# Routing stage of a graph and mixture-of-experts kernel: VectorE's work per group cut in four parts and reordered, scatter places from two products and a scan, expert weights turned one unit per group

## The reference

```
x = x + gnn(layernorm(x), edge_attr_16, edge_attr_4, ..., src, dst)   # x: 6250 x 256, 200000 edges, 8 heads
flat   = layernorm(x)
probs  = softmax(flat @ router_w.T)                                   # 8 experts
topk_probs, topk_idx = top_k(probs, 2)
topk_probs = topk_probs / (sum(topk_probs) + 1e-09)
gates  = einsum("nk,nke->ne", topk_probs, one_hot(topk_idx, 8))
h      = silu(flat @ w1[e].T) * (flat @ w3[e].T)                      # w1, w3: 8 x 682 x 256
y[e]   = h @ w2[e].T                                                  # w2: 8 x 256 x 682
x      = x + sum over e of gates[:, e] * y[e]
```

## Time and profile before

| | |
|---|---|
| median of 3 runs | 4229.73 us |
| the profiled execution, its own time | 4242.61 us |
| its span | 4240.8 us |
| the stage between loop and experts | 3059.6 to 3309.0 us of the span |
| busy share of the span: PE, PEld, DVE, ACT, POOL | 74%, 56%, 47%, 38%, 44% |
| scatters on POOL (L1298) | 98, busy 106.8 us, idle before them 131.0 us |
| weight transposes on PE (L1428) | 192, busy 50.5 us |
| router matmuls on PE (L1405) | 196, busy 45.3 us |
| granted TensorE clock in the stage | 0.50 |

### The profile page before, as it was taken

One profiled execution on the slowest core, in us unless ns is written; L12 is line 12 of the kernel. 1 busy time (PEld: TensorE's weight loads), 2 busy tenths in 40 slices (PEclk: granted clock), 3 DMA queues, 4 the chain that ended last, 5 costly groups with the idle time before them and its releaser, 6 DMA issues. The chain is left out here.

```text
span 4240.8 us, 66247 instructions
## 1 busy us (share of the span) xinstructions
PE 3155.8 (74%) x12650; PEld 2393.4 (56%) x12651; DVE 1982.3 (47%) x5336; ACT 1615.5 (38%) x3611; POOL 1861.5 (44%) x1906
## 2 busy tenths in 40 slices
PE   2532787777777777777777777777766699999997
PEld 1221665555565656555555665565555477777775
DVE  5730555555555555555555555555744122222221
ACT  2311544444444444444444444444422122222221
POOL 0005455556555555555555555555245111111111
PEclk9865667777767777777777677767755899999998
DMA  7744444444444444444444444446553321221113
GB/s 217 253 134 120 122 128 124 125 127 126 125 125 127 128 123 127 131 128 126 125 127 124 125 125 125 125 125 118 87 176 133 101 32 30 32 31 31 31 31 82
DMA packets 311626, 480.40 MB, mean 113 GB/s; under 512 B 164215, under 2 KB 239811, under 8 KB 302670
## 3 DMA queue, kind: packets, MB, share of 16 engines
q0 software_dynamic: 100848, 285.40, 27.4%
q1 hardware_dynamic: 208606, 193.39, 15.2%
q10 hardware_dynamic: 2000, 0.06, 0.0%
HBM read 408.92 MB, written 76.12 MB: 114 GB/s over the span
## 5 line engine op out<-in xcount | busy, mean ns | idle before, releaser
L838 POOL DMA_INDIRECT rows<-table,idx x1664 | 1577.9, 948 | 1141.0 <-issue 488.8
L881 PE MATMUL ps_acc<-rows,hot 128*128 128x264 f32 x3328 | 1274.3, 521 | 396.9 <-DVE acc L1169 342.9
L881 PEld LDWEIGHTS ps_acc<-rows,hot 128*128 128x128 f32 x3328 | 767.9, 255 | 535.1 <-issue 422.0
L1169 DVE TENSOR_TENSOR acc<-acc,ps_acc 128x264 f32 x832 | 356.7, 429 | 1047.0 <-remote 459.5
L866 PEld LDWEIGHTS ps_term<-er,hot_t 128*128 128x128 f32 x3328 | 619.1, 249 | 285.6 <-issue 235.6
L866 PE MATMUL ps_term<-er,hot_t 128*128 x3328 | 608.2, 314 | 125.6 <-issue 93.3
L1155 DVE TENSOR_TENSOR rows<-rows,ps_p 128x512 f32<-128x512 f32 x832 | 565.7, 680 | 2.4 <-ACT ps_p L984 0.5
L973 ACT ACTIVATE hot<-iota_row,neg_rel 128x128 f32<-128x128 f32 x1664 | 545.8, 388 | 4.8 <-PE ps_acc L881 4.6
L1713 PE MATMUL ps_h<-w,acc 128*128 x1680 | 530.8, 459 | 0.5 <-ACT acc L1632 0.5
L1625 POOL DMA_INDIRECT x_dram<-acc,to x105 | 161.8, 1541 | 755.2 <-ACT acc L1641 755.2
L948 ACT COPY e_t<-ps_e 128x128 f32<-128x128 f32 x208 | 57.5, 277 | 1003.1 <-remote 684.3
(11 more groups left out here) (264 smaller groups left out, 2960.7 us busy)
## 6 DMA issues: line engine op xcount, KB each, us to landing
dst_row<-rel_d SPq DMA_DIRECT2D x52, 1024.0 KB
rows<-table,idx POOLq DMA_INDIRECT x1664
rec<-rec_d SPq DMA_DIRECT2D x848, 24.0 KB
rec_d<-acc SPq DMA_DIRECT2D x16, 1050.0 KB
acc<-slots_x SPq DMA_DIRECT2D x105, 130.0 KB, 2.1
acc<-in_edge_attr_dram SPq DMA_DIRECT2D x16, 700.0 KB
wrow<-in_L_ffn_w_dram SPq DMA_DIRECT2D x16, 640.0 KB
table<-fo SPq DMA_DIRECT2D x49, 148.0 KB
```

The source lines that it names most:

```text
L838: pool.indirect_dma_start(rows[w][:, t, :], None, table, bass.IndirectOffsetOnAxis(ap=idx[w][:, t:t + 1], axis=0)).then_inc(gathered[w * Q ...
L881: last = pe.matmul(ps_acc[m % 2][:, 0:PW], hot[m // QI % 2][:, m % QI * G + j, :], rows[m // NI][:, tile_of(m % NI, j), 0:PW], start=(j == ...
L1169: dve.tensor_tensor(so_far, so_far, ps_acc[m % 2][:, 0:PW].rearrange("p (h d) -> p h d", h=HEADS), ALU.add).then_inc(added, 1)
```

## The change

Four things are changed, all in this stage.

1. VectorE's `normal` and `route` become `sum_up` (division, residual, statistics), `normal` (from the square root on), `choose` (softmax, picks, counts) and `send` (gates, slots). The order is `sum_up(0)`, `normal(0)`, `sum_up(1)`, and then per group `choose(g)`, `normal(g+1)`, `send(g)`, `sum_up(g+2)`. `inv` is made per group.
2. The picks are written with the experts outside (`chosen`), a scan along the seven blocks (`within`) with a zero factor at each expert's first block counts them, and the count so far is added (`so_far`). `places` has two products instead of eight, and `tally` is gone.
3. Two weight units are turned ahead of group 0, one per group, and the last seven behind group 6. ScalarE issues the weight loads, each behind the copies of the unit two before.
4. TensorE issues a group's transposes and logits, then a weight unit, then the same group's places; ScalarE runs `copies(g)`, `exps(g)`, `root(g+1)`, one `keep_weights`.

```diff
@@ GpSimd: the triangle now subtracts
-                    pool.memset(upper[:, :], 1.0).then_inc(pool_step, 1)
+                    pool.memset(not_above[:, :], 0.0).then_inc(pool_step, 1)
...
-                    pool.affine_select(out=upper[:, :], in_=upper[:, :], compare_op=ALU.is_ge, fill=0.0, base=-1,
+                    pool.affine_select(out=not_above[:, :], in_=not_above[:, :], compare_op=ALU.is_ge, fill=-1.0, base=-1,
@@ SyncE
-                        for n in of_group(g):
-                            if n + W_RING < 2 * EXPERTS:
-                                sp.wait_ge(w_ps, KC * (n + 1))
-                                load_weights(n + W_RING)
@@ ScalarE
+                    def load_weights(n):
+                        w, full, to = (w1, w3)[n % 2], (HCH - 1) * P, wrow[n % W_RING]
+                        act.dma_start(to[:, 0:HCH - 1, :], ...).then_inc(wrow_in[n % W_RING], 16)
+                        act.dma_start(to[0:HLAST, HCH - 1, :], ...).then_inc(wrow_in[n % W_RING], 16)
...
                             act.copy(w13[:, n // 2, at:at + HID], ps_w13[:, 0:HID]).then_inc(w_sb, 1)
+                        if n + W_RING < UNITS:
+                            load_weights(n + W_RING)
+                    for n in range(W_RING):
+                        load_weights(n)
                     root(0)
-                    copies(0)
-                    for n in of_group(0):
+                    for n in range(FIRST_UNITS):
                         keep_weights(n)
-                    for g in range(1, GROUPS):
-                        root(g)
-                        exps(g - 1)
+                    for g in range(GROUPS):
                         copies(g)
-                        for n in of_group(g):
-                            keep_weights(n)
-                    exps(GROUPS - 1)
+                        exps(g)
+                        if g + 1 < GROUPS:
+                            root(g + 1)
+                        keep_weights(unit_of(g))
+                    for n in last_units():
+                        keep_weights(n)
@@ TensorE
-                        pe.matmul(at, upper[:, :], hit[:, :, :], start=True, stop=False)
-                        for j in range(BC - 1):
-                            pe.matmul(at[:, j + 1:BC, :], ones[:, :], hit[:, j:j + 1, :].to_broadcast(...), start=False, stop=False)
-                        pe.matmul(at, ones[:, :], tally[:, :].unsqueeze(1).to_broadcast(wide), start=False, stop=True).then_inc(slot_ps, 1)
+                        pe.matmul(at, not_above[:, :], chosen[:, :, :], start=True, stop=False)
+                        pe.matmul(at, ones[:, :], so_far[g % 2][:, :, :], start=False, stop=True).then_inc(slot_ps, 1)
...
+                    for n in range(FIRST_UNITS):
+                        turn_weights(n)
+                    for g in range(GROUPS):
+                        turn(g * BC)
+                        for b in range(g * BC, (g + 1) * BC):
+                            if b + 1 < (g + 1) * BC:
+                                turn(b + 1)
+                            logits(b)
+                        turn_weights(unit_of(g))
+                        places(g)
                     pe.wait_ge(slot_used, GROUPS)
+                    pe.matmul(ps_s[:, 0:EXPERTS], ones[:, :], so_far[(GROUPS - 1) % 2][:, :, BC - 1], ...).then_inc(count_ps, 1)
+                    for n in last_units():
+                        turn_weights(n)
@@ VectorE
-                            dve.tensor_tensor(hit[:, :, :], pick1[:, :, :], pick2[:, :, :], ALU.add).then_inc(pick_ok, 1)
+                            step(dve.tensor_tensor(by_expert, pick1[:, :, :], pick2[:, :, :], ALU.add))
+                        step(dve.tensor_tensor_scan(flat(within[:, :, :]), flat(carry_on[:, :, :]), flat(chosen[:, :, :]), 0.0, ALU.mult, ALU.add))
+                        before = so_far[(g - 1) % 2][:, :, BC - 1:BC] if g else none[:, :, :]
+                        dve.tensor_tensor(so_far[g % 2][:, :, :], within[:, :, :], before.to_broadcast(...), ALU.add).then_inc(pick_ok, 1)
...
-                        step(dve.tensor_reduce(added_to[:, :], hit[:, :, :].rearrange("p b e -> p e b"), AX.X, ALU.add))
-                        dve.tensor_tensor(tally[:, :], tally[:, :], added_to[:, :], ALU.add).then_inc(tally_ok, 1)
...
+                    sum_up(0)
                     normal(0)
-                    for g in range(1, GROUPS):
-                        ...
-                        normal(g)
-                        route(g - 1)
-                    route(GROUPS - 1)
+                    sum_up(1)
+                    for g in range(GROUPS):
+                        choose(g)
+                        if g + 1 < GROUPS:
+                            normal(g + 1)
+                        send(g)
...
+                        if g + 2 < GROUPS:
+                            sum_up(g + 2)
```

More of the change, by code:

```diff
@@ L1233, in gnn_moe_kernel @@
             spare = sb(st, "spare", [P, 2, BC])
[L1234 to L1235 removed]
+            chosen = sb(st, "chosen", [P, EXPERTS, BC])
+            within = sb(st, "within", [P, EXPERTS, BC])
+            so_far = [sb(st, f"so_far{u}", [P, EXPERTS, BC]) for u in range(2)]
+            carry_on = sb(st, "carry_on", [P, EXPERTS, BC])
+            none = sb(st, "none", [P, EXPERTS, 1])
             slots_f = sb(st, "slots_f", [P, 2, BC])
             slots = sb(st, "slots", [P, 2, BLOCKS], I32)
[L1238 removed]
+            not_above = sb(st, "not_above", [P, P])
             pad = sb(st, "pad", [P, RW])
```

77 lines of the change are left out of this document (32 added, 45 removed).

## The result

The changed kernel takes 4197.81 us (median of 5, 4180.72 to 4209.09) against 4229.82 for the kernel before: a ratio of 0.9922 (0.9897 to 0.9948). It is 32 us faster; forecast were 62, and the time lies outside the range.

What follows compares the result with a forecast made beforehand. A cycle of waits (logits, weights, root, rows), no engine, bounds the kernel. Scatters ending at 3246.2 and weights at 3245.5 put the barrier at 3246.5 against 3309.0: 62.5 us gained, 4168 us; range 4160 to 4190.

Steps and rivals of the forecast that it cites:

- period taken: Time from choose to choose: 18.8 us, taken between VectorE's 17.7 and TensorE's 19.1 with the delay.
- the delayed hand-over: Between engines while scatters run: 3.9 us, read from one group of the kernel before and kept in TensorE's period.
- TensorE's period: TensorE's cycle per group: 15.2 us from the steps, 19.1 us with the 3.9 us of delay.
- two thirds of each burst of scatters ran without it: Argument against the slower rival, where delay holds while POOL is busy: 52 us slower, 4282 us, chance 0.03.
- Scatters without a pause: POOL needs 20.0 us per group against 18.8 us, so 98 scatters run unbroken from 3100.7 to 3236.3.
- the rival in which the delay strikes harder: 3.9 us in each group plus 2.5 us on VectorE: period 21.6 us, gain 47.5 us, 4182 us, chance 0.25.
- The rival of the ports: VectorE instructions with two SBUF inputs held by scatters, 6 us a group: period 23.7 us, 4196 us, chance 0.05.
- the first logits: Start of the stage: root at 3073.9, four half units to 3081.3, seven blocks of 8.75 us, first choose at 3090.6.
- the parts of VectorE: Per group: choose 5.1, normal 2.5, send 2.2 and sum_up 7.9 us, together 17.7 us.
- the root that waits for nothing: ScalarE's square root has no weight copies ahead of it; VectorE's wait for it near zero.
- the tail: Seven weight units behind the count at 3211.3, 4.88 us each, loads covered, ending at 3245.5.
- GpSimd's drain: End of the stage: 9.9 us from the last scatter's end to the barrier kept, including the 8.07 us DRAIN.

Runs made afterwards that it cites:

- r1: The changed kernel again, unaltered, on a chip where the kernel before takes 3662.26 us: 3614.64 us, ratio 0.9854.
- e4: The changed kernel with one 0.2 us GpSimd operation on an idle tile behind each scatter: 4184.62 us, ratio 0.9882 to the kernel before.
- e2: The changed kernel with two 0.2 us GpSimd operations on an idle tile behind each scatter: 4220.37 us, ratio 0.997 to the kernel before.
- e3: The changed kernel with a 4.2 us GpSimd rest ahead of each group's first scatter, from group 1 on: 4191.90 us, ratio 0.9899 to the kernel before.

## Why the prediction was wrong

Its steps, from the stage's start, beside the changed kernel on the first chip and on one without late hand-overs:

| | forecast | first chip | r1 |
|---|---|---|---|
| first `choose` | 31.0 | 29.5 | 29.2 |
| VectorE's own period | 17.7 | 17.6 | 17.7 |
| period taken, or mean of the six | 18.8 | 23.8 | 17.4 |
| `choose` of group 6 | 142.1 | 172.3 | 133.6 |
| end of the last scatter | 176.7 | 199.9 | 174.5 |
| barrier | 186.9 | 217.5 | 184.4 |

- **The step that failed** is the size of the delayed hand-over, a term of TensorE's period. I read 3.9 us in one group of the kernel before, kept it as a constant of each group ("I keep this: 19.1 us") and took 18.8. It is no constant: here it begins 16 to 17 us into an unbroken burst and goes on, with hand-overs up to 16.2 us late, until GpSimd pauses. In the kernel before each burst was some 20 us long and only its end was late; the change joins the bursts, two groups long. Over the 17.7 it measured 7.3 and 8.7 us in the second and fourth distance and 18.7 in the last (21.4 over the 15.0 us of r1, where no `sum_up` stands in that distance). That makes `choose` of group 6 come 30.2 us late and the barrier 30.6, nearly the whole of the miss. I had written beside it that "two thirds of each burst of scatters ran without it", which was the clue: I held it for a sign that the delay is small, and it was its onset. The trace of the kernel before had more: I read the first 64 gathers of the edge loop, and not the waits marked "remote" behind them.
- **Scatters without a pause** from 3101 to 3236 failed with it: GpSimd waited 27.5 us for slots in three pauses. On r1 it never waited after the first.
- **The way it went** was nearest to the rival in which the delay strikes harder, but its 21.6 us a group and 4182 us were still too small. The rival of the ports, whose 4196 us come near the time, was wrong, and that the time came near it is chance: the scan took 0.27 us beside the scatters, `choose` 5.1 us as forecast, and VectorE's period 17.6. What the prediction takes from the Trainium skill, "SBUF — State Buffer", section "Who interferes with whom", is wider than the page, which has the block for a whole instruction for VectorE's two-port modes and lets an instruction with two SBUF inputs contend only with a GpSimd instruction that reads SBUF. The trace again shows one direction: the scatter at 3107.75 takes 2.00 us instead of 0.96 beside VectorE's product at 3106.90, which keeps its 2.03.
- **What held:** the first logits, the parts of VectorE, the root that waits for nothing, the tail (36.7 us for seven units against 34.2), GpSimd's drain, the forecast of the barrier to 2.5 us on r1.

The drain in the changed kernel on the first chip and in r1, and the table load on the first chip, beside the earlier trace rows:

```profile
L1284 POOLq DRAIN  x1: 8068/8068/8068, 3251.5 to 3251.5; - x1
```

```profile
L1284 POOLq DRAIN  x1: 8068/8068/8068, 2677.0 to 2677.0; - x1
```

```profile
3078.96 1.28 ACT L1350 ACT_TABLE_LOAD   x1
3080.26 0.30 ACT L1350 ACTIVATE rstd<-mv,eps 128x7 f32<-128x7 f32 x1
```

On the first chip the last burst is again one of 14 scatters, behind a pause of 16.7 us; in r1 all 98 came without a pause, and the drain is the same length. 0.02 us lie between the load's end and the root. The Trainium skill, "ScalarE: Activation LUTs", section "What ACT_TABLE_LOAD costs", adds a drain of 1.38 us to a switch; no row here shows it, and the measurement decides.

A scatter's row ends after 0.96 us whether hand-overs are late or not. The Trainium skill, "Perfetto Trace Analysis", section "DMA Instruction — SWDGE (GPSIMD)", says why such a row tells nothing of what is still to be done: its end is the last descriptor written, and the end of the moves and each DMA engine's semaphore write come later. The trace agrees: in e4 `normal` waited until 3172.18 for scatters of which the last row had ended at 3167.29, 4.9 us before; in e2 the same way took 1.6 to 1.7 us. That the late hand-overs are such a backlog is my reading and was not shown, nor what it is that queues up. Against the simplest form of it, r1 has the same 4.9 us (2602.09 to 2606.94) and no late hand-over.

## What to carry to other kernels

A delay that shows only at the end of a burst isn't a constant to be carried over: ask from which point of the burst it begins and what a longer burst would do, before a change joins bursts. Where GpSimd issues indirect DMAs for over 15 us in a row, read the time between a product's end and the copy that waits for it alone; if it comes to microseconds, a pause of 0.2 us behind each DMA can be worth more than it costs, and buffers held longer are its price. And time such a kernel on more than one chip.

## What the runs showed of the hardware

- Two kinds of chips: 4225 to 4233 us and 3662 to 3663 us for the same kernel, at the same 1.2 GHz of TensorE's clock in the stage (granted 0.50 on both). The 567 us lie in the edge loop, with its gathers each 1.59 or 1.28 us. No experiment shows that late hand-overs are the whole of it; the clock granted there differs as well (0.70 and 0.79), and which follows from which is open.
- On the slower kind hand-overs of 0.04 us take 5.3 us after some 17 us of scatters 1.27 us apart (up to 16.2 in the changed kernel), not at 1.47 us apart for 152 us. A pause of 4.4 us cleared them for another 17 us in the changed kernel, while with e3's rests of 4.2 us they came back 9 us into the third burst. What differs between the chips stays open.
- A 128x128 memset of 0.22 us between two scatters costs 0.20 us, seven in a row 1.85.
